# Another order of the last batch and the second part, on four engines, in a perceiver layer kernel

## What is computed

```python
x = x + cross_attention(layernorm(x), ctx)   # 16 heads of 16, keys and values from 1601 rows
x = x + self_attention(layernorm(x))         # 16 heads, 64 tokens, rotary tables, biases
x = x + moe(layernorm(x))                    # 8 experts, top 1, 128 places each, gate = softmax
```

## Time and profile before

| | |
|---|---|
| median of 3 runs | 702.0 us (701.88 to 703.59) |
| span of the profiled execution | 699.7 us |
| PE busy | 671.0 us (96%) |
| DVE busy | 552.5 us (79%) |
| ACT busy | 443.4 us (63%) |
| POOL busy | 549.0 us (78%) |

### The profile page before, as it was taken

The page is one execution under the profiler, slowest core; times in us unless marked ns, Lnnn a source line. Parts: engine busy times, 40 slices in busy tenths (PEclk is TensorE's granted clock), DMA queues, the critical chain, the costliest instruction groups (busy, mean ns, idle before and its releaser), DMA issues.

```text
span 699.7 us, 21737 instructions
## 1 busy us (share of the span) xinstructions
PE 671.0 (96%) x8632; PEld 507.2 (72%) x8681; DVE 552.5 (79%) x1138; ACT 443.4 (63%) x885; POOL 549.0 (78%) x374
## 2 busy tenths in 40 slices
PE   4799999999999999999999999999999998899897
PEld 2556786877777877787778777877777786677673
DVE  4697877868888878778787868787868788888867
ACT  2446766666666666676767666767675787665830
POOL 7759999999699889798989789889788786723422
PEclk9999999999999999999999999999999999999999
DMA  8587055454445454545353645363543450000212
GB/s 309 143 213 214 27 138 162 99 155 97 150 113 155 105 164 92 160 107 165 93 165 84 178 102 159 85 187 89 169 97 104 100 164 4 2 2 9 91 69 91
DMA packets 45610, 84.20 MB, mean 120 GB/s; under 512 B 8668, under 2 KB 28420, under 8 KB 45508
## 3 DMA queue, kind: packets, MB, share of 16 engines
q1 hardware_dynamic: 43896, 80.13, 41.9%
q0 software_dynamic: 912, 2.14, 1.0%
q10 hardware_dynamic: 704, 0.55, 0.3%
HBM read 36.89 MB, written 6.55 MB: 62 GB/s over the span
## 4 chain that ended last, share of the span: by engine, by line
PE 82%; DVE 5%; DMA 5%; SPq 2%; issue 2%; POOL 2%; ACT 2%; ACTq 0%; DVEq 0%; POOLq 0%
PE ps_kv L821 17%; PE ps_kv L812 16%; PE ps_score L872 12%; PE ps_out L896 12%; PE ps_front L844 12%; PE ps_score L920 2%; SPq L502 2%; DMA kstack<-khigh 2%; PE ps_out L912 1%; DMA cbuf<-in_ctxT 1%; PE ps_kv L783 1%; DMA wq_sb<-in_wqT 1%; PE ps_front L920 1%; PE ps_front L853 1%; PE ps_kv L920 1%
## 5 line engine op out<-in xcount | busy, mean ns | idle before, releaser
L637 POOL TENSOR_TENSOR plow<-prob 128x1024 bf16<-128x1024 f32 (+1 forms) x198 | 372.1, 1898 | 58.8 <-ACT prob L1242 56.3
L1511 DVE TENSOR_REDUCE maxes<-ps_front 128x1 f32<-128x512 f32 (+1 forms) x416 | 267.1, 666 | 57.2 <-PE ps_front L844 53.9
L1242 ACT ACTIVATE prob<-ps_score 128x512 f32<-128x512 f32 (+1 forms) x416 | 236.2, 598 | 71.0 <-PE ps_score L872 61.9
L872 PE MATMUL ps_score<-qstack,kstack 98*128 98x128 bf16 (+1 forms) x1664 | 150.5, 219 | 0.8 <-ACT prob L1242 0.5
L844 PE MATMUL ps_front<-kstack,qstack 96*128 96x512 bf16 (+1 forms) x512 | 145.4, 333 | 2.7 <-DMA kstack<-khigh 1.9
L872 PEld LDWEIGHTS ps_score<-qstack,kstack 98*128 98x128 bf16 (+1 forms) x1664 | 112.1, 98 | 33.7 <-ACT prob L1242 1.9
L896 PE MATMUL ps_out<-vstack,prob 128*128 128x65 bf16 (+1 forms) x1664 | 113.6, 194 | 0.7 <-POOL plow L637 0.3
L821 PE MATMUL ps_kv<-w_hi,cbuf 128*128 128x256 bf16 (+1 forms) x402 | 109.7, 273 | 0.9 <-DVE vstack L1501 0.9
L1494 DVE SCALAR_TENSOR_TENSOR klow<-ps_kv,bcol,khigh 128x512 bf16<-128x512 f32 (+1 forms) x123 | 76.8, 629 | 42.5 <-ACT khigh L1220 42.0
L821 PE MATMUL ps_kv<-w_hi,clow 128*128 128x256 bf16 (+1 forms) x402 | 109.5, 272 | 0.0
L821 PE MATMUL ps_kv<-w_lo,cbuf 128*128 128x256 bf16 (+1 forms) x402 | 109.5, 272 | 0.0
(11 more groups left out here) (290 smaller groups left out, 858.7 us busy)
## 6 DMA issues: line engine op xcount, KB each, us to landing
kstack<-khigh SPq DMA_DIRECT2D x256, 100.1 KB, 2.2
cbuf<-in_ctxT SPq DMA_DIRECT2D x15, 1601.0 KB, 7.2
kstack<-klow SPq DMA_DIRECT2D x128, 100.1 KB, 2.2
qstack<-q_blocks SPq DMA_DIRECT2D x48, 64.0 KB, 2.3
q_blocks<-qbd SPq DMA_DIRECT2D x16, 128.0 KB, 2.0
cbuf<-in_weT SPq DMA_DIRECT2D x2, 1024.0 KB, 7.8
slot_x<-att_all SPq DMA_DIRECT2D x8, 128.0 KB, 7.1
vstack<-slot_x SPq DMA_DIRECT2D x4, 256.0 KB, 3.6
```

Of the source, the lines that this page charges most:

```text
L637: nc.gpsimd.tensor_tensor(plow[slot][0:n, :], prob[slot][0:n, :], p_high(slot, 0, HP * P)[0:n], ALU.subtract).then_inc(plow_gps, 1)
L872: mm = nc.tensor.matmul(ps_score[0:nn, h % NSB, j * P:(j + 1) * P], kstack[par][0:98, hp, n0:n0 + nn], qstack[par][0:98, q_at(hp), :], sta ...
L1242: nc.scalar.activation(prob[slot][0:nn, e * 512:e * 512 + 512], ps_score[0:nn, h % NSB, :], ACT.Exp)\
L1511: nc.vector.reduce_max(maxes[:, hp:hp + len(unit), n], ps[:, 0:len(unit) * nn].rearrange("p (h k) -> p h k", k=nn), AX.X).then_inc(m_free, 1)
```

## The change

The four strings end in another order. The same letters stand in them, each as often as before; everything ahead of the last two or three lines is untouched. On GpSimd the order was `p195 p196 r0 r1 t0 Z0 b2 p197 t1 r2 b3 I0 b4 t2 b5 I1 I2 b6 r3 ...` and is `p195 r0 p196 r1 Z0 t0 b2 p197 t1 r2 b3 b4 r3 R0 t2 t3 r4 t4 I0 b5 b6 ...`, with I1, I2 and I3 moved behind s1, t7 and I2, and Y2 behind g4. On VectorE it was `... p2 p3 p4 X0 D0 X1 G0 D1 N0 p5 G1 L0 p6 N1 T0 L1 p7 p8 T1 p9 X2 ... N2 a14 M2 M3 U2 L2 U3 W0` and is `... p2 X0 D0 G0 p3 p4 X1 D1 G1 N0 N1 p5 L0 L1 p6 T0 p7 p8 a14 T1 X2 ... N2 p9 M2 M3 L2 U2 W0 U3`. On TensorE `H0 s411 s412 w404 w405 s413 J0 H1 s414 w406 w407 s415 T0 J1 A2 V0` became `H0 H1 s410 s411 w404 w405 s412 J0 s413 V0 s414 w406 w407 s415 T0 J1 A2`, and `W0 J2 V2` became `W0 V2 J2`.

```diff
--- before.py
+++ after.py
@@ PE_PROGRAM @@
-     "wwsmsKmsmsKwmmwsswmwwmswKwsmKmsmKmswsmmKmssmwwmwsmwswmsmKmwswsmwmsKmsmwswmsZmwswwsAwswwwwssOswsAwsww"
-     "ssOswswwswswsswwswssswwsHsswwsJHswwsTJAVOTSVwwwwwSPPwHwwWJVAP2PTOoWSA2HOoJPPhVTHlWVJS2AToOhSPPhlWPl2"
-     "PHAocWOJAV2OHToJhSHhlTlVJcVPTPSWSPP2Wo2PPoxhWlxghcxglx2gcogFhFlFFFFcFFFFFF", 1),
+     "wwsmsKmsmsKwmmwsswmwwmswKwsmwKmsmKsmsKmsmwwwsmswmwwsmsmwsmsmKmsmwsKmwsmwwwsmmZmwswswswwwsssAswswsOss"
+     "wwwAswwswsOsswwwswsswswHHsswwsJsVswwsTJAOTSVwwwwwSPwPHwwWVJP2ATPOoWSA2HOoVhPJHlPTJVWS2ATohOSlPPhWlP2"
+     "AHPoOcWJAV2HOToJShTHhlVlJPPcTSVWSP2PoWPP2xohWxlghxgclx2gocgFhFlFFFcFFFFFFF", 1),
@@ ACT_PROGRAM @@
-     "KeKeeeKKeeeeKeeeeKeKKeeeKeeKeKeKeKKeKReeRKeeeKeeKeeKeeKeKeeeKeKeeeeeZKeeeKeReeReeeAeeeeeAeeeeeeeeeee"
-     "eeHeeeHeeBATVTBVEEPPHEEVA2PTPBAH2EEPfPHViBTV2ABTEEfPPifEEPi2PAHlAV2HBTffHiTiBElVEVPTPBEEPP2EE2PPxhfi"
-     "xylhfxyixl2yyfhil", 1),
+     "KeKeeeKKeeeeKeeeeKeKKeeeKeeKeKeKeKKeKReReKeeeKeeKeeeKeeKKeeeKeKeeeeeeeZKeeKeeRReeeeeeeAeeeeeAeeeeeee"
+     "eHHeeeeeeBATVTBVEEPPHEVE2APPBTA2HEfEHVPPTiBV2ABTfEEPPEifEiP2AlHPA2VHBTfHfTiiVEEBlPPBTVEE2PPEEP2xPfhi"
+     "xylxhfyi2lxyyfhil", 1),
@@ DVE_PROGRAM @@
-     "KmmKmmmKmmmKmKmmKmmmKmKmKKmKmKmKmvmKmmmKKmmmmmaKmmKmKmmmKmKmKmmmKKmmKmKmKmmKvmmKmmKmKmmmmKmmmKmmmmmm"
-     "KmKmmmKmaZpvppppXDXGDNpGLpNTLppTpXDGMMUUNaMMULUWvTXDxGWdNMgMLUUnXDGTNxLadgWTnMMUxUdXgDMnMUGUWN1xL3WX"
-     "DdGTNgXDLGxdngNTnMMLU1UT3MMUUWMMUUWxdgnxdqg1nqWq31qxd3gnyyyy1yyffy3fyyffyyy", 1),
+     "KmmKmmmKmmmKmKmmKmmmKmKmKKmKmKmKmvmKmmmKKmmmmmaKmmKmKmmmKmKmKmmmKKmmKmKmKmmKvmmmmKmKKmmmKammmmKmmmmm"
+     "mKmmKmmKmZpvppXDGppXDGNNpLLpTppaTXDGMMUUNpMMLUWUvTXDxGdWNgMMULXnDGUxNdTLagTnWMMUUxdXgDMnUMGUWN1xLXDG"
+     "W3NdTgXLDxGdgnTNnMMULU1T3MMUUWMMUUxdWgnqxdgWnq1q31qxdgn3yy1yyyy3yffyyfyffyy", 1),
@@ POOL_PROGRAM @@
-     "pcpcppppqpppppppcppcpccppppcpppcppcpppcpppppcppppppppccpcpppppppppppppppppbbpprrtZbptrbIbtbIIbrRrRbt"
-     "tRrrRtrsRsIsttssRRYYRggggYg", 1),
+     "pcpcppppqpppppppcppcpccppppcpppcppcpppcpppppcppppppppccpcpppppppppppppppppbbprprZtbptrbbrRttrtIbbRRr"
+     "rsbRttrRsIssstIIRYRYRgggggY", 1),
```

## The result

The changed kernel takes 703.04 us (median of 20 runs, 701.45 to 705.20) against 701.65 (20 runs of the kernel before, 699.17 to 703.59): ratio 1.0021, 95% interval 1.0012 to 1.0030. The forecast was 699.6 with a range of 697.2 to 701.8. The change costs 1.4 us where a gain of 2.4 was expected.

What follows compares the result with a forecast made beforehand. TensorE, 96% busy, was taken as the bound, with VectorE's order setting the time around the last batch's end. -0.7 - 1.0 - 0.7 = -2.4 took the span from 699.7 to 697.3; plus 2.3 gave 699.6 us, range 697.2 to 701.8.

Steps and rivals of the forecast that it cites:

- Step five: 612 to 650 us, dense on TensorE: regrouped units have inputs long ready, GpSimd's room covers later I's; 0, 0.4 either way.
- Steps one to four: Up to L2, around the last batch's end: J2's 0.90 wait goes, T1 starts 0.3 later; taken as -0.7 us.
- step two: N0 and N1 together ahead of p5: N1, held by memsets, ends near 588.1, 3.7 us sooner; p5 ends 1.5 later.
- Step one: Before 586 us, reordered units: p196 still ends at 585.71, nothing gained or lost, 0.4 us either way.
- the first rival: Around N1: it gets the port after one memset, waiting about 0.5 instead of 1.5; 698.6 or 697.3 us; chance 0.22.
- Step six: 650 to 661 us: nothing gained at S7; W6's 0.51 wait covered, -0.5; last slots before the first F, -0.5.
- step seven: The F pairs: F6's 0.43 wait for y4 goes, with what lay hidden in the tail of the product before; -0.7.
- the second rival: Late stretch: waits only move to S7, P14 or another pair; 0.3 gained instead of 1.7; 701.0 us; chance 0.25.
- The third rival: Around N1: GpSimd holds on until p197 ends, N1 ends near 592.8; 702.3, up to 704.4 us; chance 0.11.

Runs made afterwards that it cites:

- the experiment with b7: The changed kernel with b7 put ahead of the indirect DMA s0 on GpSimd: 702.31 us, ratio 1.0003 to the kernel before.
- the experiment with V6: The changed kernel with V6 put ahead of h4 on TensorE: 702.71 us, ratio 1.0009 to the kernel before.
- both edits: The changed kernel with one I moved behind t1 and b7 ahead of s0, both on GpSimd: 698.89 us, ratio 0.9955 to the kernel before.
- the experiment with t0 ahead: The kernel with both edits, with t0 also put ahead of the memsets Z0 on GpSimd: one run, 700.06 us, beside 698.89 without it.
- the first experiment: The changed kernel with one I moved behind t1 on GpSimd, so none stands between s1 and s2: 700.31 us, ratio 0.9981 to the kernel before.

## Why the prediction was wrong

**Step five failed**, and with it the sign. The prediction put the dense stretch from 612 to 650 us at "0, with 0.4 either way" and took the moved I's to be covered because GpSimd had room. It asked whether GpSimd had room, not at which moment VectorE's units would meet GpSimd's. s1, with an I behind it as before, now starts 0.26 us ahead of n4 and no longer 0.15 after it, and n4 takes 2.88 instead of 0.41; b7 behind s0 held X7; J6 and h4 together waited 2.54 us where TensorE had no such wait, and part of TensorE's clock went with it. The two edits that take the I and b7 out of these two places, and nothing else, turn 703.04 into 698.89. The last sentence of the prediction had named "GpSimd's I units there hold up VectorE's normalisations" among what would make it wrong; it had no price and no chance in the list of rivals, which is the real omission. A rival on the slower side was there, but at another place (N1).

How the loss divides between the wait and the clock shows only roughly. Of the changed kernel's 20 runs the 9 with a mean granted clock of 0.998 or 0.999 took 701.45 to 702.62 us and the 11 with 0.995 or 0.997 took 702.99 to 705.20. None of the 20 has 1.000, and the profiled run of the experiment with b7 has 0.998 with a fall in it (0.50 in the window from 650 to 652). So these runs part a longer fall from a shorter one, and the longer costs between one and two microseconds more. Nearest to no fall come three runs of the experiment with V6, at a mean clock of 1.000: 702.12 to 702.79 us, against 698.35 to 699.46 with both edits. They have no trace; if n4 is held in them as in the profiled one, the waits alone eat the lead.

**Steps one to four were too small, for N1 in step two.** Step one stayed within its 0.4: p196 began at 583.76, in the earlier trace rows at 583.78, net 0.27 sooner. The forecast for the four was -0.7; W1 came 1.84 sooner net. The mis-sized term is N1 in step two. It was put at 1.6, ending near 588.1 behind the memsets; VectorE's and GpSimd's rows of the changed kernel:

```profile
586.38 0.61 DVE L1585 TENSOR_SCALAR klow<-klow,mv,rs 128x256 f32<-128x256 f32 x1 [0.45 <-POOL rs L687]
586.91 1.20 DVE L1481 TENSOR_TENSOR plow<-prob 128x1024 bf16<-128x1024 f32 x1
...
591.24 4.56 DVE L1481 TENSOR_TENSOR plow<-prob 128x1024 bf16<-128x1024 f32 x2
...
596.61 0.69 DVE L1603 TENSOR_TENSOR kstack<-ps_front,cst 128x512 f32<-128x512 f32 x1
```

```profile
586.30 1.18 POOL L659 MEMSET kstack<- 128x544 f32 x2
587.42 0.55 POOL L659 MEMSET vstack<- 128x544 f32 x1
```

N1 takes 0.61 with the memsets beside it, p5 its usual 1.20, p5 ends at 588.1 (forecast 589.3), T1 starts at 596.61 (597.7): the first rival, one microsecond sooner, was right, and N1 was held for even less than its 0.9. The row it argued from, N1 of before, was read rightly as held through t0 and the memsets (the experiment with t0 ahead brings the 2.28 back), but wrongly carried over to an order without t0 in front. p5 beside the memsets agrees with the Trainium skill (SBUF — State Buffer, Who interferes with whom), that two SBUF inputs contend with GpSimd's reads and not with its writes alone. N1 held by t0 and the memsets in turn, and n4 held from before I1's record began, are not what its clause of one whole instruction for the engine that issues first would give from the recorded starts.

p7 and p8 (4.56, forecast 4.4) and T1 to L2 (596.61 to 604.46, 7.85, forecast 8.17) came as put. The waits of 1.33 in front of H1 and 0.90 in front of J2 are gone, that of T1 (1.11) stayed, against the earlier trace rows.

**Step six did not come, step seven did.** Both are read in the kernel with both edits, where step five no longer covers them. From W1 to F0 the net lead goes from 1.82 to 1.69, so step six gave nothing (0.1 was lost) instead of 1.0: W6's wait of 0.51 is gone, but S7, with 0.38, now waits 0.85, and by the trace for ScalarE:

```profile
654.47 1.09 PE L995 MATMUL ps_front<-kstack,vstack 64*64 64x256 f32 x16 [0.85 <-ACT kstack L1275]
```

That is the second rival (what W6 no longer waits for is waited for at S7), right for step six. From F0 to F11 the lead grows from 1.69 to 2.26: 0.6 for the 0.7 of step seven, with no wait in front of F6. In that kernel the order is worth 2.26 net and 3.0 by the medians (interval 2.0 to 4.3), near the 2.4 of the sum, but by terms that differ: 1.8, -0.1, 0.6 for 0.7, 1.0, 0.7. That the total fits is luck. The third rival, N1 held for over 4 us, didn't occur.

## What to carry to other kernels

When the orders of two engines that were seen to hold each other up move against each other, list for each unit what the other engine runs at the moment it now becomes ready, and price it by rows; room in the queue says nothing of that. Here an I stood behind s1 in both kernels, and less than half a microsecond in n4's start against s1's decided between 0.41 and 2.88. A row that shows an operation held belongs to the order of both engines around it, and holds for the new order only if the same operation starts in front. A stretch that is dense and whose sum was put at nothing is where a forecast is most exposed: each moved unit in it wants a row of its own.

## What the runs showed of the hardware beyond what was expected

A VectorE normalisation of 256 columns that became ready a quarter of a microsecond into an indirect DMA on GpSimd took 0.41 us when another DMA followed, 0.98 when an addition of 0.73 us followed (also with I1 right behind that), and 2.88 when a subtraction of 1.90 us followed. In the kernel before it began 0.15 us ahead of such a DMA with such a subtraction behind, and took 0.41.

In five of the six profiled executions here in which TensorE waited 0.8 us or more for a held normalisation (1.94, 1.26, 1.97, 0.84 and 1.43 us), its granted clock then fell to 0.50, and the windows add up to 3 to 7 us at that level, though TensorE was busy by then. In the sixth, the kernel before, H1's 1.33 us for N1 were followed by no fall, and in the five executions without such a wait the clock stayed at 1.00 there. That the wait causes the fall is likely, but was not tested by itself, and the length of a wait alone does not decide it: besides H1's, T1's 1.1 us were followed by a fall in a single execution, that with V6 ahead of h4. Nor is this wait needed for a lower mean clock: four of the 11 runs of the first experiment, whose profiled execution has n4 free, show 0.995 to 0.997.
